# State space stage of a perceiver layer: one more product by C on GpSimd, input products and convolutions moved, the previous step's last pair ended later

## The reference, cut to what matters

```python
xz = einsum('bld,ed->ble', Z, in_proj_w)
x, z = split(xz, 2)
x = silu(causal_dw_conv(x, conv_w, conv_b))          # 4 taps
dt, Bm, Cm = split(einsum('bld,ed->ble', x, x_proj_w), [32, 48])
dt = softplus(einsum('blr,dr->bld', dt, dt_proj_w) + dt_proj_b)
deltaA = exp(dt[..., None] * A); deltaBx = dt[..., None] * Bm * x[..., None]
h = deltaA_t * h + deltaBx_t                          # over the tokens, 16 states
y_t = sum over states of h * C_t                      # the product by C
y = (y + x * D) * silu(z);  return y @ out_proj_w.T
```

## Time and profile before

| | us |
|---|---|
| median of 3 runs | 3929.63 (3928.04 to 3933.65) |
| the profiled execution | 3929.74 |
| its span | 3928.0 |
| state space, first scan to last scan | 2442 to 3419 |
| one step of it | 122.8 |

### The profile page before, as it was taken

One profiled execution on the slowest core, in us unless ns is written; L12 is line 12 of the kernel. 1 busy time (PEld: TensorE's weight loads), 2 busy tenths in 40 slices (PEclk: granted clock), 3 DMA queues, 4 the chain that ended last, 5 costly groups with the idle time before them and its releaser, 6 DMA issues. The chain is left out here.

```text
span 3928.0 us, 83651 instructions
## 1 busy us (share of the span) xinstructions
PE 3795.5 (97%) x34848; PEld 2798.4 (71%) x34848; DVE 2814.0 (72%) x2970; ACT 1793.0 (46%) x3565; POOL 1292.0 (33%) x610
## 2 busy tenths in 40 slices
PE   8999999999999999999999998999999999799999
PEld 6778777777878878877777776554555544288887
DVE  5567667667667667667767766999999999855444
ACT  2334324324424424424423436778877788532222
POOL 1111121021021021111111111899999999830000
PEclk9999999999999999999999998999999999999999
DMA  4110111011011010011011013012120122120000
GB/s 148 49 44 29 39 45 34 34 55 32 26 54 32 26 55 32 29 52 42 29 41 45 26 55 118 19 52 65 59 60 22 55 65 80 34 79 33 33 17 27
DMA packets 96918, 183.74 MB, mean 47 GB/s; under 512 B 8465, under 2 KB 12945, under 8 KB 96562
## 3 DMA queue, kind: packets, MB, share of 16 engines
q1 hardware_dynamic: 96562, 178.27, 14.1%
HBM read 152.82 MB, written 25.43 MB: 45 GB/s over the span
## 5 line engine op out<-in xcount | busy, mean ns | idle before, releaser
L244 POOL TENSOR_TENSOR c_lo<-c_raw,c_hi 128x2048 fp32r<-128x2048 f32 x64 | 295.1, 4611 | 1926.5 <-DVE c_hi L346 1926.5
L407 DVE TENSOR_REDUCE max_parts<-scores 128x2 f32<-128x1024 f32 x512 | 603.6, 1221 | 212.7 <-PE scores L572 212.7
L434 DVE TENSOR_TENSOR prob_sums<-prob_sums,probs 128x1024 f32<-128x1024 f32 x480 | 566.8, 1223 | 115.9 <-ACT probs L319 115.9
L1012 POOL TENSOR_TENSOR b_drive<-b_dt_u,b_bc 128x1024 f32<-128x1024 f32 x256 | 601.4, 2361 | 114.9 <-PE b_y L1457 69.0
L319 ACT ACTIVATE probs<-scores 128x512 f32<-128x512 f32 x1024 | 529.2, 604 | 215.8 <-PE scores L603 214.3
L1457 PE MATMUL b_y<-b_drive,b_ident 128*128 128x512 f32 x1024 | 491.1, 610 | 80.9 <-DVE b_drive L1329 40.2
L1318 DVE TENSOR_TENSOR_SCAN b_decay<-b_decay,b_drive 128x1024 f32<-128x1024 f32 x210 | 480.3, 2287 | 15.5 <-ACT b_decay L1190 13.2
L304 ACT ACTIVATE k_hi<-scores,bk_sb 128x512 fp32r<-128x512 f32 x256 | 176.7, 690 | 604.1 <-PE scores L528 604.1
L312 ACT COPY v_sb<-scores 128x512 f32<-128x512 f32 x240 | 141.2, 588 | 635.3 <-PE scores L528 635.3
L1190 ACT ACTIVATE b_decay<-b_dt,b_a 128x254 f32<-128x254 f32 x1024 | 426.8, 464 | 0.4
L1457 PEld LDWEIGHTS b_y<-b_drive,b_ident 128*128 128x128 f32 x1024 | 188.6, 192 | 314.1 <-issue 173.1
(11 more groups left out here) (305 smaller groups left out, 6535.9 us busy)
## 6 DMA issues: line engine op xcount, KB each, us to landing
c_raw<-in_ctx SPq DMA_DIRECT2D x64, 1024.0 KB, 5.2
b_bc<-bc_scratch SPq DMA_DIRECT2D x128, 256.0 KB, 4.3
c_w_raw<-in_mlp_w SPq DMA_DIRECT2D x16, 512.0 KB, 3.6
q_scratch<-v_sb SPq DMA_DIRECT2D x4, 1024.0 KB, 4.3
q_raw<-q_scratch SPq DMA_DIRECT2D x16, 256.0 KB, 5.2
q_raw<-in_x SPq DMA_DIRECT2D x16, 256.0 KB, 2.8
x_scratch<-q_raw SPq DMA_DIRECT2D x16, 256.0 KB, 5.8
attn_scratch<-attn_out_sb SPq DMA_DIRECT2D x16, 256.0 KB, 2.0
```

Of the source, the lines that this page charges most:

```text
L244: pool.tensor_tensor(c_lo[:, slot], c_raw[:], c_hi[:, slot].bitcast(F32), ALU.subtract).then_inc(c_lo_ready, 1)
L407: dve.tensor_reduce(max_parts[:, g, 2 * pair:2 * pair + 2, s], max_banks[:, 2 * pair:2 * pair + 2, :], AX.X, ALU.max).then_inc(max_taken, 1)
L434: dve.tensor_tensor(part, part, probs[:, u % 4], ALU.add).then_inc(summed, 1)
L1012: pool.tensor_tensor(drive[:, m % 4], dt_u[:, 2 * p:2 * p + 2, :].unsqueeze(1).to_broadcast([P, SG, 2, T]), bc[:, g, 0].unsqueeze(2).to_br ...
```

## The change

- `POOL_C` gets unit 4 in front, so in the seven steps that are not the last the product by C of unit 4 goes from VectorE to GpSimd, behind the drive of unit 6.
- `POOL_RSTD` goes from 7 to 6, and `norm_rstd` is issued ahead of the product by C of its turn instead of behind it.
- The fourth x input product goes from behind unit 12 to behind unit 10. The z input products go from behind units 13, 14, 15, 17, 22, 23, 25, 26 to 12, 13, 15, 17, 23, 24, 25, 26.
- The taps go from ScalarE's units 11, 12, 14, 16 to 10, 11, 13, 16, the convolutions from VectorE's units 11, 12, 13, 15 to 10, 11, 12, 15.
- At unit 0 (`END_BEHIND`) VectorE ends the previous step's last pair behind the product by C of unit 0, not ahead of it.
- Behind Silu of u, ScalarE runs a one-column Exp into a helper tile `table_taker`.

```diff
-    PE_IN_X = (5, 7, 8, 8, 9, 9, 12, 12)
-    PE_IN_Z, PE_OUT = (13, 14, 15, 17, 22, 23, 25, 26), (27, 29, 31)
-    POOL_DT_U1, POOL_DT_H1, POOL_DT_U2, POOL_DT_U3, POOL_RSTD, POOL_OUT = 0, 3, 6, 8, 7, 11
+    PE_IN_X = (5, 7, 8, 8, 9, 9, 10, 10)
+    PE_IN_Z, PE_OUT = (12, 13, 15, 17, 23, 24, 25, 26), (27, 29, 31)
+    POOL_DT_U1, POOL_DT_H1, POOL_DT_U2, POOL_DT_U3, POOL_RSTD, POOL_OUT = 0, 3, 6, 8, 6, 11
-    ACT_LOG1, ACT_SQUARES, ACT_XN, ACT_XN_T, ACT_SCALE, ACT_TAP, ACT_U = 1, 8, 6, 7, 13, (11, 12, 14, 16), 17
+    ACT_LOG1, ACT_SQUARES, ACT_XN, ACT_XN_T, ACT_SCALE, ACT_TAP, ACT_U = 1, 8, 6, 7, 13, (10, 11, 13, 16), 17
-    DVE_X1, DVE_CONV = (2, 4), (11, 12, 13, 15)
+    DVE_X1, DVE_CONV = (2, 4), (10, 11, 12, 15)
+    END_BEHIND = (0,)
-    POOL_C, POOL_C_LAST = (10, 11, 12, 14, 17, 19), (9, 12, 26, 28)
+    POOL_C, POOL_C_LAST = (4, 10, 11, 12, 14, 17, 19), (9, 12, 26, 28)
...
+                    if not last and m == POOL_RSTD:
+                        norm_rstd(j)
                     if m - C_BEHIND in on_pool(i):
                         c_product(i, m - C_BEHIND)
...
-                        if m == POOL_RSTD:
-                            norm_rstd(j)
...
                 ins.then_inc(u_ready, 1)
+
+                act.activation(table_taker[:], zeros[:, 0:1], ACT.Exp)
...
+            def end_last_pair(i, par, p, first):
+                if p > 0:
+                    end_pair(i, par, p - 1)
+                elif not first:
+                    end_pair(i - 1, 1 - par, pairs - 1)
...
-                    if g == 0:
-                        if p > 0:
-                            end_pair(i, par, p - 1)
-                        elif not first:
-                            end_pair(i - 1, 1 - par, pairs - 1)
+                    if g == 0 and m not in END_BEHIND:
+                        end_last_pair(i, par, p, first)
                     if m not in on_pool(i):
...
+                    if m in END_BEHIND:
+                        end_last_pair(i, par, p, first)
```

More of the change, by code:

```diff
@@ L745, in mamba @@
         minus_half = sb("b_minus_half", [P, group])
-        wait_taker = sb("b_wait_taker", [P, 1])
+        wait_taker, table_taker = sb("b_wait_taker", [P, 1]), sb("b_table_taker", [P, 1])
         shift_ln = sb("b_shift_ln", [P, group])
```

## The result

The changed kernel takes 3954.83 us (median of 4 runs, 3944.37 to 3956.39) against 3929.17 for the kernel before in the same comparison: a ratio of 1.0056, 95% interval 1.0045 to 1.0068. It is slower by 0.56%, where 3932.9 was forecast with a range to 3941. The profiled execution of the changed kernel took 3944.37 us (span 3942.3), the one of before 3929.74 (span 3928.0).

What follows compares the result with a forecast made beforehand. VectorE was nearest to the bound (117.77 of 122.78 us a step), with three engines within a fifth of it, in a ring. Terms -0.6 + 0.9 - 1.39 + 5.1 - 1.41 + 0.59 = +3.2 gave 3932.9 us; range 3915 to 3941.

Steps and rivals of the forecast that it cites:

- Units 24 to 28: Moving z product 2 by one unit removes the 0.64 wait at 24 but delays the scan of unit 28: +0.89 us.
- Units 0 to 2: Pair ended behind the product by C: the 1.06 wait mostly becomes a ScalarE wait; scan 2 is +0.59 us late in all.
- Units 4 to 9: Unit 4's product on GpSimd, behind the waiting deviation, delays TensorE's sum of unit 4: +0.94 us a step, scan 9 +1.53 in all.
- Units 15 to 20: The 0.81 wait goes and scan 18 comes 1.36 earlier, but scan 20 only 0.68 earlier: -0.68 us, not -1.82.
- The rival on TensorE's clock: Clock falls behind TensorE's new stand before unit 4's sum: 0.79 us more a step, 3938.4 in 7 steps; 20% with other GpSimd lateness.
- The sum: All steps added up: -0.6 + 0.9 - 1.39 + 5.1 - 1.41 + 0.59 = +3.2 us, forecast 3932.9.
- The full step: One full step of the state space: 0.59 + 0.94 - 0.68 = +0.85 us, +5.1 for 6 steps.
- The start up to the first pair's end: First step: front -0.6 us, units 4 to 9 0.9, units 15 to 20 -0.68, longer wait at unit 16 -0.71.
- The last step: The last step of the state space was to start 0.59 us later.
- the first step's fall at unit 12: Unit 12's sum takes 2.77 us in place of 1.96, lengthening the wait at unit 16, which goes: another -0.71.
- The load that costs more: Rival: the Exp load moved ahead of the skip copy also holds ScalarE 1.38 us: +9.7 in 7 steps, 3942.6; 3%.
- The helper does nothing: Rival: the helper's Exp load is placed elsewhere; within 0.5 us a step of the forecast, counted as no change; 3%.

Runs made afterwards that it cites:

- the best version: Not singled out in the text; lowest median 3921.55 us (0.9979): changed kernel, no helper, z halves at 12, 14, 15, 17, 23, 23, 25, 26, deviation behind unit 4's product, x half later.

## Why the prediction was wrong

**Units 24 to 28** (+0.89): right. The waits changed by -0.64 + 1.52 = +0.88.

**Units 0 to 2** (+0.59 in all, so -0.30 for this part): right in kind. 1.06 went and 0.53 came before scan 2, where I had 0.76; so -0.53.

**Units 4 to 9** (+0.94): right. The product gives back 1.13 to 1.26, 0.64 at unit 7 and 1.41 at unit 8 come; undone, it is 0.88. The mechanism is shown by the kernel with the deviation behind the product.

**Units 15 to 20** (-0.68): the walk of VectorE's scans was right, -0.81 - 0.59 + 0.62 = -0.78 in a step at full clock. **Here is the step that failed.** I wrote that without the z half the sum of unit 15 is early, and that the skip copy is later by the helper. I did not put the two together on TensorE. It is done early, its next sum waits for a copy that has become later, and so it stands 2.97 us where it stood 0.28. I treated that as free, because TensorE was not the late engine there, and for VectorE it is free as long as the clock holds. But what stands behind the sum is the product for dt, B and C, on which the decay of unit 20 hangs with nothing slack. That term, the fall of TensorE's clock behind the stand at unit 16, stands in the sum at nothing; measured, it is up to 2.9 us a step and 10.4 in the profiled execution.

**The rival on TensorE's clock** had the mechanism and two things wrong. I placed it at unit 4, the one stand that I had worked out; that is 1.31 us, and in no full step but the first did the clock fall there. And I priced it by the sum of unit 12 in the first step, as 0.79 a step, though the same rows have 1.41 lost in the second step. That price counts the four passes only, and not all of them at the low clock. Here the clock stayed down over the product behind them too, and the 20 instructions lost 2.85. I should have gone through every stand of TensorE that the edit makes or lengthens. The skip copy's wait was to be had from the earlier trace rows: Silu's end, the load of 1.28, the copy, against the end of the last input product.

**The sum.** Without the falls at unit 16 the profiled execution would be at 3934, near my 3932.9, but that is partly chance. The full step is +0.50 and not +0.85, mostly by units 0 to 2 (0.23) and 15 to 20 (0.10). The six steps without these falls give +1.6 where I had 5.1 - 1.4 = +3.7. The start up to the first pair's end gives +1.76 where I had -0.6 + 0.9 - 0.68 - 0.71 = -1.1; here the rival's place was right, once. In the first step GpSimd's product lets TensorE stand 4.31 us before the sum of unit 4, where its stand before the change was one of 3.02 before the sum of unit 5, at full clock behind it. Now the clock falls:

```profile
2469.82 5.11 PE L1465 MATMUL b_y<-b_drive,b_ident 128*128 128x512 f32 x8 [4.31 <-POOL b_drive L990]
```

The last step is 2.24 shorter where I had it start 0.59 later; TensorE's clock falls at several sums there in both kernels, and I did not separate these. And 3.1 lie behind the stage, most of it where the clock came back later than in the execution of before. One term is read a little wrong too: the first step's fall at unit 12 is put at 0.71 as the excess of its sum (2.77 in place of 1.96 is 0.81); 0.71 is the excess of the wait behind it, 1.52 in place of 0.81.

**The runs above the profiled one.** With 2.9 us for each of seven steps instead of 10.4 in all, 3944.4 becomes 3954.3, and the other three runs of the changed kernel lie at 3953 to 3956. They have no trace, so this fits and is not shown.

**The load that costs more** (3%): no. Two switches follow each other in the rows of the helper above: each load takes 1.28 us and what needs it starts 1.29 and 1.30 after the load's start. The Trainium skill, page "ScalarE: Activation LUTs", section "What ACT_TABLE_LOAD costs", has a drain of about 1380 ns beside the load of 1283 ns; by that the helper would have held the skip copy 1.4 longer. Here too the trace agrees with the load and shows no drain.

**The helper does nothing** (3%): its load does move, as the waits before scan 18 show (0.42 in place of 1.01), but alone it gained nothing. The rival had this right for another reason: what the helper won at scan 18 came back at scan 20 and at the pair's end of unit 24.

Open: why a stand of 2.98 us is harmless in three steps and costs 2.9 in later ones; the same holds for the one of 2.63 at unit 12. Open too is how much of the median's 0.56% is falls and how much is unit 4's product: the slower runs have no trace, and taking either away brings the median back. That the stand at unit 16 is needed for the falls there is shown by the kernel with the z half at 14. Which of its steps fall is not explained, and it moves with edits elsewhere: leaving out unit 4's product gave falls at unit 16 in steps 1, 2, 4, 6 and 7 in place of 4 to 7.

## What to carry to other kernels

When work moves away from ahead of an in-order wait, look at what its engine does in the hole: on TensorE a stand is not free even where no one waits for it, since the clock can fall and the next instructions may lie on the path; so list every stand that an edit makes or lengthens, and price a fall over all that follows until the clock is back. On an engine with a fixed order, put the product that others wait for ahead of the instruction that waits itself: this exchange on GpSimd, together with the z half back at 14, turned a loss of 0.4 to 0.6% into a gain of 0.2%. And a table load taken out of one wait is not yet a gain: here, alone, it came back whole at the next two waits, and ahead of the copy that restarts the PSUM bank it lengthened TensorE's stand from 2.17 to 2.97.

## What the runs showed of the hardware

- TensorE's granted clock fell behind stands of 1.86 to 2.98 us in some steps and not in others of the same execution, and a longer stand did not always cost more (3.54 for four passes behind 1.86, 1.99 behind 2.98). In the first step a stand of 3.02 before the sum of unit 5 left the passes at 1.98 in the kernel before and doubled them to 3.78 in the changed kernel without unit 4's product. Behind 2.97 us the four passes took 3.78 us in place of 1.99, 1.9 times as long, at a granted clock of 0.50, the 1.2 GHz level, and part of the next product did too (4.72 in place of 3.67, granted clock 0.77). Behind the stands of 1.26 and 1.31 us in the full steps they took their usual time.
- The end of the kernel, which none of the edits touches, takes 499.4 to 500.1 us in five profiled executions and 503.0 to 504.2 in nine. In the five, TensorE is back at full speed 5.3 to 6.2 us behind a stand of 5.47 us, in the nine some 10 to 11.5 us behind it. The 3.3 between the two is 0.08% of the time, some four tenths of what the best version gained.
- Two table loads in a row cost 1.28 us each with no further gap.
